# A selective scan cut in two: the decays of one state of each pair move to PSUM, and the edge weights share a bank with C's copies

## The chip, the cores and the metric

The kernel runs on one core of a Trainium2 chip. The metric is the device time of one execution in microseconds (us), as the median of a few runs. Kernels are compared on the same chip.

## What is computed

The reference is one graph layer followed by a mixture of experts, over 6250 nodes of 256 features and 200,000 edges. Only two parts of it run in the stretch that the change touches, side by side.

The first is the graph attention sum: for every edge a row of the projected table is fetched by its source node, scaled by a weight for each of four heads, and added to the row of its target node.

```python
e = leaky_relu(s_src[src] + s_tgt[tgt], 0.2)
agg = segment_sum(proj[src] * attn[:, :, None], tgt)
```

The second is a selective scan ("mamba") over the nodes, sorted by degree, with 256 channels and 16 states:

```python
dA = exp(dt[:, :, None] * A)
dBx = (dt * xc)[:, :, None] * Bm[:, None, :]
h = dA_t * h + dBx_t          # for each t in order
y_t = h @ C_t
```

## The kernel before

`streams` (L510) runs both parts interleaved. The nodes are cut into 28 chunks of 224. A chunk takes 16 **slots**, one for each state. The position of a slot in its chunk is `at` (0 to 15). Two states make a pair: the even slot holds the scan of both, the odd slot what follows from it. The edges come in **edge pairs** of 512 edges (`S` in the code); three slots of every four (`at % 4` = 1, 2, 3) have one, so a chunk has 12. Four edge pairs form a group (`GU = 4`), whose logits and weights are computed together, in the slots with `at` = 1, 6 and 11. `run` writes out 32 slots (two chunks) and loops over them. The order of the work on each engine is written by hand, and engines meet only through semaphores.

What each engine does in a slot, in its order of issue:

- **VectorE**, `slot` L1185: at `at` = 2 `give_out`; `add` (L620: adds the sums of edge pair S-3 from PSUM `fl_ps` to `ACC`); `scale` (L610: multiplies the gathered rows of S-1 by the weights in PSUM `fl_pw`); in a slot that begins a group the first step of `logits` (L585); then in an even slot `scan` (L1124, one instruction over both states, 2 x 2 x 225 = 900 elements: decays `mb_dA`, inflow `mb_dB`, state `mb_h`), in an odd slot `read_out` (L1134: `mb_h` times C from PSUM `fl_pc`, into `mb_hc`); the rest of `logits` (L589 to L602); `prepare` for the next chunk; and in an odd slot `inflow` (L1111: `mb_dB` of the next pair, from PSUM `fl_pb`).
- **ScalarE**, `slot` L1309: `one_hot` (L628, L633), `keep_last` in odd slots (L1239, L1242), `weights` (L648), `give_out`, `prepare`, `decay(M + 2)` (L1251, two instructions of 224 elements for one state), `keep_turned` (L643, L644), and in a slot that begins a group `weights_again` (L654, writes `fl_pw`).
- **TensorE**, `slot` L1440: in an even slot `copies_c` (L1363: spreads two rows of C over all partitions into `fl_pc`), in an odd slot `copies_b` (L1353, the same for B into `fl_pb`); then `edges_tensor`: `gather_sums` of S-2 (L683), `turn` (L663) and `spread` (L670); in an odd slot `sum_up` (L1375); then `give_out` and `prepare` for the next chunk: at `at` = 2 the projection for z (L1382), at `at` = 4 the convolution (L1407).
- **GpSimd**: nothing but the gathers, four indirect DMAs for each edge pair (L567), as far ahead as buffers are free. SyncE brings indices and rows.

All eight PSUM banks are in use: `fl_ptx`, two `fl_ps`, `fl_pw`, `fl_pb`, `fl_pc`, `fl_py`, `fl_pm`. The decays live in SBUF in `mb_dA` with four buffers, one for each state.

Of the kernel before, what the change touches and what calls it, by code (L numbers as in the profile page):

```python
# [7 lines left out]
ALU = mybir.AluOpType  # L8
ACT = mybir.ActivationFunctionType
# [6 lines left out]
P = 128  # L16
# [5 lines left out]
KD = D // P  # L22
NH, FO = 4, 64
ROW = D + NH
SC = 512
NJ = SC // P
# [4 lines left out]
GU = 4  # L31
# [5 lines left out]
NS, DR, CONV = 16, 16, 4  # L37
N2 = NS // 2
TC, RB = 224, 112
# [67 lines left out]
def two_states(m):  # L107

    return Slot(m.i, m.n // 2, BODY // 2)


def pair_beside(m):

    at = m.n % 4 - 1
    return Slot(m.i, G_INTRO + m.n // 4 * 3 + at, GB) if at >= 0 else None
# [395 lines left out]
def streams(nc, sem, w, a, dram, srcT, parts, tile_of):  # L511
# [12 lines left out]

        "weights", "set", "rate", "x", "xT", "xT_sb", "in", "z_in", "z_sb", "history", "xc",
        "bx", "bx_hi", "bx_rest", "bx_mid", "bx_mid_sb", "bx_lo", "dt_row", "dt_in", "v", "abs", "e", "ln", "series",
        "dt", "u", "B", "C", "dA", "dB", "h", "h0", "hc", "y", "skip", "gated", "o", "o_sb", "oT", "oT_sb", "stored")}
    gathered = [sem(f"fl_gathered{g}") for g in range(2 * GU)]
    index = [sem(f"fl_index{h}") for h in range(2)]
    brought = [sem(f"fl_dst{g}") for g in range(4)]  # L530
    early = lambda v, least: isinstance(v, int) and v < least
    with ExitStack() as ctx:
# [19 lines left out]
        pX = pTX[:, words:words + NJ * SPREAD].rearrange("p (j s) -> p j s", s=SPREAD)  # L552
        pS = [ps(f"fl_ps{b}", [P, 512])[:, 0:ROW] for b in range(2)]
        pW = ps("fl_pw", [P, 512])
        weight = pW[:, 0:GU * NJ * NH].rearrange("p (c h) -> p c h", h=NH)
        ACC = w["ACC"]

        def free(pool, p):
# [46 lines left out]
        def scale(dve, p):  # L605
            q, n = p.number, p.n
            g, at = n // GU % 2, slice(n % GU * NJ, (n % GU + 1) * NJ)
            dve.wait_ge(s["weight"], p.of(GU) + 1)
            rows = G[g][:, at, 0:D].rearrange("p j (h f) -> p j h f", h=NH)
            nc.vector.tensor_tensor(rows, rows, weight[:, at, :].unsqueeze(3).to_broadcast([P, NJ, NH, FO]),  # L610
                                    ALU.mult).then_inc(s["scaled"], 1)

        def add(dve, p):
            q = p.number
            k = dve.value_load(tile_of[0:1, bass.ds(q, 1)], min_val=0, max_val=NT - 1)
            at = ACC[:, bass.ds(k, 1), :].rearrange("p o d -> p (o d)")
            if not early(q, 1):
                dve.wait_ge(s["added"], q)
            dve.wait_ge(s["summed"], q + 1)
            nc.vector.tensor_tensor(at, at, pS[p.n % 2], ALU.add).then_inc(s["added"], 1)  # L620
# [29 lines left out]
        def weights_again(act, p):  # L650

            if not early(p.number, 1):
                act.wait_ge(s["scaled"], p.number)
            nc.scalar.activation(weight, DM[:], ACT.Exp).then_inc(s["weight"], 1)  # L654
# [47 lines left out]
        def edges_tensor(pe, S):  # L702
            if not early(S.number, 2):
                gather_sums(pe, S - 2)
            turn(pe, S + GU)
            spread(pe, S + GU)
# [104 lines left out]
        with ExitStack() as part:  # L811
# [14 lines left out]
            first = G_COUNT + 5  # L826
# [101 lines left out]
        with ExitStack() as part:  # L928
# [19 lines left out]
            H0, ZERO = sb("mb_h0", [P, N2, 2, KD]), sb("mb_zero", [P, 1])  # L948
            LOWER = sb("mb_lower", [P, 1])
            Y, O, OR = sb("mb_y", [P, KD, TC]), sb("mb_o", [P, KD, TC]), sb("mb_or", [RB, TS, D])  # L950
            pB, pC = ps("fl_pb", [P, 2, TC]), ps("fl_pc", [P, 2, TC])
            pY, pM = ps("fl_py", [P, KD, TC]), ps("fl_pm", [P, 512])
            wide = lambda t: t[:, 0:KD * TC].rearrange("p (k t) -> p k t", k=KD)
            xs = dram["sorted_x"].rearrange("(c r p) d -> c p r d", p=RB, r=TS)
# [124 lines left out]
            def _(dve):  # L1079
# [19 lines left out]

                nc.vector.memset(LOWER[:], float(-np.log(ROOT)))  # L1100
                nc.vector.memset(dA[:, :, :, 0:1], 0.0).then_inc(s["set"], 1)

                def inflow(p):

# [9 lines left out]
                def scan(p):  # L1114

                    m, n = p.number, p.n
                    dve.wait_ge(s["dB"], m + 1)
                    dve.wait_ge(s["dA"], 2 * m + 2)
                    if not early(m, 1):

                        dve.wait_ge(s["h0"], 2 * m)
                        dve.wait_ge(s["hc"], m)
                    line = lambda t: t.rearrange("p s k t -> p (s k t)")
                    nc.vector.tensor_tensor_scan(line(H[:]), line(dA[:, n % 2 * 2:n % 2 * 2 + 2]), line(dB[:]), ZERO[:, 0:1],  # L1124
                                                 ALU.mult, ALU.add).then_inc(s["h"], 1)

                def read_out(p):
                    m, n = p.number, p.n
                    dve.wait_ge(s["h"], m + 1)
                    dve.wait_ge(s["C"], m + 1)  # L1130
                    if not early(m, 2):

                        dve.wait_ge(s["y"], m - 1)
                    nc.vector.tensor_tensor(HC[:, n % 2], H[:, :, :, 1:], pC[:].unsqueeze(2).to_broadcast([P, 2, KD, TC]), ALU.mult  # L1134
                                            ).then_inc(s["hc"], 1)

                def prepare(c, b, at):
# [47 lines left out]
                def slot(M, S):  # L1185
                    n, c = M.n, M.of(NS)
                    at, b = n % NS, n // NS % 2
                    two = two_states(M)
                    if at == 2 and not early(c, 1):
                        give_out(c - 1, 1 - b)  # L1190
                    if S:
                        add(dve, S - 3)
                        scale(dve, S - 1)
                    steps = logits(dve, S) if S and S.n % GU == 0 else None
                    if steps:
                        next(steps)
                    if at % 2:
                        read_out(two)
                    else:
                        scan(two)  # L1200
                    if steps:
                        next(steps)
                        next(steps)
                        next(steps)
                        next(steps)
                    prepare(c + 1, 1 - b, at)
                    if at % 2:
                        inflow(two + 1)
# [6 lines left out]
                        prepare(0, 0, at)  # L1215
                inflow(two_states(Slot(0, 0)))
                nc.vector.memset(dB[:, :, :, 0:1], 0.0).then_inc(s["set"], 1)
                dve.wait_ge(s["set"], 13)
                run(dve, slot)
                add(dve, pair(PAIRS - 3))  # L1220
                scale(dve, pair(PAIRS - 1))
# [8 lines left out]
            def _(act):  # L1230
                act.wait_ge(s["weights"], 144)
                nc.scalar.activation(AE[:], A[:], ACT.Exp).then_inc(s["rate"], 1)
                act.wait_ge(s["set"], 12)

                def keep_last(p):

# [7 lines left out]
                def decay(p):  # L1244

                    m, n = p.number, p.n
                    if not early(m, 4):

                        act.wait_ge(s["h"], two_states(p).number - 1)
                    for k in range(KD):  # L1250
                        ins = nc.scalar.activation(dA[:, n % 4, k, 1:], DT[:, n // NS % 2, k, :], ACT.Exp,  # L1251
                                                   scale=A[:, k, n % NS:n % NS + 1])
                    ins.then_inc(s["dA"], 1)

# [54 lines left out]
                def slot(M, S):  # L1309
                    n, c = M.n, M.of(NS)  # L1310
                    at, b = n % NS, n // NS % 2
                    if S:
                        one_hot(act, S + (GU + 1))
                    if at % 2:
                        keep_last(two_states(M))
                    if S and S.n % GU == 0:
                        weights(act, S)
                    if not early(c, 1):
                        give_out(c - 1, at)
                    prepare(c + 1, 1 - b, at)  # L1320
                    decay(M + 2)
                    if S:
                        keep_turned(act, S + GU)
                    if S and S.n % GU == 0:
                        weights_again(act, S)

                for k in range(SCAT):
# [12 lines left out]
            def _(pe):  # L1340
# [16 lines left out]
                def copies_c(p):  # L1357

                    m, n = p.number, p.n
                    if not early(m, 1):  # L1360
                        pe.wait_ge(s["hc"], m)
                    for r in range(2):
                        mm = nc.tensor.matmul(pC[:, r, :], SEL[:, NS + 2 * (n % N2) + r, :], PARTS[:, n // N2 % 2, :],  # L1363
                                              start=True, stop=True, skip_group_check=True)
                    mm.then_inc(s["C"], 1)
# [74 lines left out]
                def slot(M, S):  # L1440
                    n, c = M.n, M.of(NS)
                    at, b = n % NS, n // NS % 2
                    two = two_states(M)
                    if at % 2:
                        copies_b(two + 1)
                    else:
                        copies_c(two)
                    if S:
                        edges_tensor(pe, S)
                    if at % 2 and not early(M.number, 2):  # L1450
                        sum_up(two - 1)
                    if not early(c, 1):
                        give_out(c - 1, at)
                    prepare(c + 1, 1 - b, at)
# [862 lines left out]
```

## Time and profile before

| | |
|---|---|
| median of 3 runs | 3823.23 us (3822.45 to 3824.71) |
| profiled execution, own time | 3830.27 us |
| its span, first to last instruction | 3828.5 us |
| mean granted TensorE clock | 0.898 of full speed |
| 28 chunks of slots | from about 912 to 2872 us of the span |

The profile is of one execution. In a row of grouped instructions stand the line, the engine, the operation, what it writes and reads, how many, and then busy time in us, the mean of one in ns, and the idle time of the engine just before them with what ended it. In a row of the timeline stand the start and the duration in us, and in brackets the idle time just before, where there was any. Consecutive VectorE rows overlap a little: the next one starts some 0.08 us before the recorded end of the one before.

### The profile page before, as it was taken

The page shows a single profiled execution, that of the slowest core. Times are in us where ns is not written, and L with a number is a line of the kernel's source. Part 1 is how long each engine was busy: PE and PEld are TensorE (multiplying, and loading weights), DVE is VectorE, ACT ScalarE, POOL GpSimd, SP SyncE. Part 2 cuts the span into 40 slices and gives each one's busy share as a digit, 9 for nine tenths or more (in the row PEclk, how much of TensorE's full clock was granted, in tenths as well). Part 3 has the DMA queues.
Part 4 walks back from the last instruction along what each step waited for, and adds up shares of the span by engine and source line. Part 5 has one row for each costly group of instructions (what it writes and reads, how often), then busy time and mean ns, then how long its engine had stood idle before and what let it go on. Part 6 is the DMA issues. An engine that isn't in the chain of part 4 may idle for free. (4 is left out here: it accounts for less than half of the span.)

```text
span 3828.5 us, 60997 instructions
## 1 busy us (share of the span) xinstructions
PE 2897.5 (76%) x16306; PEld 2157.1 (56%) x16307; DVE 2661.2 (70%) x4225; ACT 2163.9 (57%) x4819; POOL 2649.2 (69%) x2119
## 2 busy tenths in 40 slices
PE   6465566517888788887888888888883889659998
PEld 5455455415565565565665655656652455448887
DVE  6577466625988988989888888899893788511111
ACT  2322377716777677777676776777772665412222
POOL 2788788877777777777777777777773477424443
PEclk9788777768899999999999999999996999879999
DMA  7333444454444444544444444444465243157775
GB/s 225 105 83 84 133 106 107 115 172 131 118 124 121 124 118 117 127 120 122 124 118 120 123 118 126 121 120 124 120 112 136 56 106 99 69 133 143 143 144 105
DMA packets 295783, 460.78 MB, mean 120 GB/s; under 512 B 59431, under 2 KB 217880, under 8 KB 295288
## 3 DMA queue, kind: packets, MB, share of 16 engines
q0 software_dynamic: 116320, 279.61, 30.8%
q1 hardware_dynamic: 179224, 178.73, 16.6%
q14 instruction: 180, 1.47, 0.1%
q8 instruction: 59, 0.97, 0.1%
HBM read 394.01 MB, written 63.43 MB: 119 GB/s over the span
## 5 line engine op out<-in xcount | busy, mean ns | idle before, releaser
L567 POOL DMA_INDIRECT el_g<-table,el_ix x1344 | 1546.7, 1151 | 412.4 <-issue 392.9
L683 PE MATMUL fl_ps<-el_g,el_oh 128*128 128x260 f32 x3520 | 959.0, 420 | 255.2 <-DVE el_g L610 207.2
L683 PEld LDWEIGHTS fl_ps<-el_g,el_oh 128*128 128x128 f32 x3520 | 697.3, 209 | 370.5 <-DVE el_g L610 215.1
L567 POOL DMA_INDIRECT el_g<-table,eg_src x436 | 592.8, 1360 | 155.2 <-issue 125.9
L610 DVE TENSOR_TENSOR el_g<-el_g,fl_pw 128x1024 f32<-128x1024 f32 x440 | 533.5, 1213 | 22.2 <-ACT fl_pw L654 22.1
L1124 DVE TENSOR_TENSOR_SCAN mb_h<-mb_dA,mb_zero,mb_dB 128x900 f32<-128x900 f32 x224 | 468.1, 2090 | 51.2 <-ACT mb_dA L1251 30.7
L1375 PE MATMUL fl_py<-mb_hc,ident 128*128 128x448 f32 x896 | 405.0, 576 | 0.5 <-DVE mb_hc L1134 0.5
L1251 ACT ACTIVATE mb_dA<-mb_dt,mb_a 128x224 f32<-128x224 f32 x900 | 382.7, 475 | 35.3 <-issue 21.2
L628 ACT ACTIVATE el_away<-el_dst,el_less 128x512 bf16<-128x512 bf16 x445 | 321.1, 721 | 108.3 <-DMA el_dst<-dst_rows 81.3
L2258 POOL DMA_INDIRECT out<-ex_y,ex_to x112 | 174.2, 1555 | 279.3 <-DVE ex_y L2217 254.5
L643 ACT CAST el_oh<-fl_ptx 128x512 f32<-128x512 bf16 x444 | 253.6, 571 | 190.8 <-PE fl_ptx L670 185.6
L663 PE MATMUL fl_ptx<-el_ident,el_oht 128*128 128x128 bf16 x1776 | 183.9, 230 | 183.3 <-ACT el_sx L644 167.3
L633 ACT ACTIVATE el_oht<-el_away 128x512 bf16<-128x512 bf16 x445 | 280.3, 630 | 36.2 <-issue 5.4
L663 PEld LDWEIGHTS fl_ptx<-el_ident,el_oht 128*128 128x128 bf16 x1776 | 139.5, 103 | 283.4 <-issue 155.0
L1111 DVE TENSOR_TENSOR mb_dB<-mb_u,fl_pb 128x896 f32<-128x896 f32 x225 | 242.5, 1078 | 46.8 <-PE fl_pb L1353 46.8
L2217 DVE TENSOR_TENSOR ex_y<-ex_py,ex_b 128x512 f32<-128x512 f32 x56 | 38.8, 692 | 333.0 <-PE ex_py L2179 333.0
L648 ACT ACTIVATE el_g<-el_dm 128x64 f32<-128x64 f32 x110 | 28.2, 256 | 424.6 <-DVE el_dm L601 424.4
L620 DVE TENSOR_TENSOR ACC<-ACC,fl_ps 128x260 f32 x440 | 182.7, 415 | 115.9 <-PE fl_ps L683 78.1
L1134 DVE TENSOR_TENSOR mb_hc<-mb_h,fl_pc 128x896 f32<-128x896 f32 x224 | 241.6, 1078 | 0.0
L585 DVE TENSOR_REDUCE el_s<-el_sx 128x128 f32<-128x384 f32 x110 | 67.6, 615 | 233.7 <-DMA el_g<-table,eg_src 171.3
L2232 ACT COPY ex_xt<-ex_px 128x512 f32<-128x512 f32 x56 | 32.8, 586 | 345.2 <-PE ex_px L2153 345.2
L1363 PE MATMUL fl_pc<-mb_parts,mb_sel 96*128 96x224 bf16 x448 | 84.9, 272 | 167.0 <-DVE mb_hc L1134 167.0
(306 smaller groups left out, 5509.0 us busy)
## 6 DMA issues: line engine op xcount, KB each, us to landing
el_dst<-dst_rows SPq DMA_DIRECT2D x446, 128.0 KB, 3.4
ex_w<-in_moe_W SPq DMA_DIRECT2D x56, 512.0 KB, 3.4
el_g<-table,el_ix POOLq DMA_INDIRECT x1344, 3.0
ex_x<-routed_x SPq DMA_DIRECT2D x56, 257.0 KB, 2.8
el_g<-table,eg_src POOLq DMA_INDIRECT x436, 2.8
mb_x<-sorted_x SPq DMA_DIRECT2D x30, 224.0 KB
table<-px_tr SPq DMA_DIRECT2D x7, 910.0 KB, 9.6
el_g<-in_x SPq DMA_DIRECT2D x7, 896.0 KB, 8.0
```

Of the source, the lines that this page charges most:

```text
L567: pool.indirect_dma_start(out=G[b // GU][:, b % GU * NJ + j, :], out_offset=None, in_=dram["table"], in_offset=bass.IndirectOffsetOnAxis(a ...
L610: nc.vector.tensor_tensor(rows, rows, weight[:, at, :].unsqueeze(3).to_broadcast([P, NJ, NH, FO]), ALU.mult).then_inc(s["scaled"], 1)
L628: nc.scalar.activation(AWAY[:], DST[:, n % 4, :], ACT.Abs, bias=LESS[:, 0:1]).then_inc(s["away"], 1)
L633: nc.scalar.activation(OHT[:, n % RO, :], AWAY[:], ACT.Relu, bias=1.0, scale=-1.0).then_inc(s["hot"], 1)
L643: nc.scalar.copy(OH[:, n % (2 * GU)], pT)
L663: nc.tensor.transpose(pT[:, j, :], OHT[:, n % RO, j * P:(j + 1) * P], I16[:])
L683: mm = nc.tensor.matmul(pS[n % 2], OH[:, n % (2 * GU), j, :], G[n // GU % 2][:, n % GU * NJ + j, :], start=j == 0, stop=j == NJ - 1)
L1111: nc.vector.tensor_tensor(dB[:, :, :, 1:], wide_u, pB[:].unsqueeze(2).to_broadcast([P, 2, KD, TC]), ALU.mult).then_inc(s["dB"], 1)
L1124: nc.vector.tensor_tensor_scan(line(H[:]), line(dA[:, n % 2 * 2:n % 2 * 2 + 2]), line(dB[:]), ZERO[:, 0:1], ALU.mult, ALU.add).then_inc(s[ ...
L1134: nc.vector.tensor_tensor(HC[:, n % 2], H[:, :, :, 1:], pC[:].unsqueeze(2).to_broadcast([P, 2, KD, TC]), ALU.mult).then_inc(s["hc"], 1)
L1251: ins = nc.scalar.activation(dA[:, n % 4, k, 1:], DT[:, n // NS % 2, k, :], ACT.Exp, scale=A[:, k, n % NS:n % NS + 1])
L1375: mm = nc.tensor.matmul(pY[:], w["ident"][:], HC[:, n % 2, r], start=first and r == 0, stop=last and r == 1)
```

## The change

Five edits, all in this stretch:

1. The edge weights (`fl_pw`) move to the upper half of a bank, and C's copies to its lower half. The bank that is freed holds `pA`, one buffer of decays for the first state of each pair.
2. `decay` writes the first state of a pair to `pA` in PSUM and the second to `mb_dA` in SBUF (two buffers). Since `pA` is single, the order becomes `decay(M + 3)` in even slots and `decay(M + 1)` in odd ones, and the first state's decay waits for the first half of the scan that read `pA` last.
3. The scan is two instructions of 450 elements: the first reads its decays from `pA`, the second from `mb_dA`.
4. On TensorE `copies_c` moves from the front of the even slot to behind `edges_tensor`, and waits until the `scale` of the same slot is done (and, after a group's first pair, until its weights are written).
5. VectorE waits for C's copies before `scale` in odd slots, and ScalarE waits before `weights_again` for C's copies (even slots) or for `read_out` (odd slots).

```diff
-        weight = pW[:, 0:GU * NJ * NH].rearrange("p (c h) -> p c h", h=NH)
+        weight = pW[:, 2 * TC:2 * TC + GU * NJ * NH].rearrange("p (c h) -> p c h", h=NH)
...
-            pB, pC = ps("fl_pb", [P, 2, TC]), ps("fl_pc", [P, 2, TC])
+            pB, pC = ps("fl_pb", [P, 2, TC]), pW[:, 0:2 * TC].rearrange("p (r t) -> p r t", r=2)
+            pA = ps("fl_pa", [P, 512])[:, 0:1 * KD * (1 + TC)].rearrange("p (s k t) -> p s k t", s=1, k=KD)
...
-                    line = lambda t: t.rearrange("p s k t -> p (s k t)")
-                    nc.vector.tensor_tensor_scan(line(H[:]), line(dA[:, n % 2 * 2:n % 2 * 2 + 2]), line(dB[:]), ZERO[:, 0:1],
+                    line = lambda t: t.rearrange("p k t -> p (k t)")
+                    nc.vector.tensor_tensor_scan(line(H[:, 0]), line(pA[:, 0]), line(dB[:, 0]), ZERO[:, 0:1],
+                                                 ALU.mult, ALU.add).then_inc(s["first"], 1)
+                    nc.vector.tensor_tensor_scan(line(H[:, 1]), line(dA[:, n % 2]), line(dB[:, 1]), ZERO[:, 0:1],
                                                  ALU.mult, ALU.add).then_inc(s["h"], 1)
...
                     if S:
                         add(dve, S - 3)
+                        if at % 2:
+                            dve.wait_ge(s["C"], two.number + 1)
                         scale(dve, S - 1)
...
-                    if not early(m, 4):
-
-                        act.wait_ge(s["h"], two_states(p).number - 1)
+                    if n % 2:
+                        to = dA[:, n // 2 % 2]
+                        if not early(m, 4):
+
+                            act.wait_ge(s["h"], two_states(p).number - 1)
+                    else:
+                        to = pA[:, 0]
+                        if not early(m, 2):
+
+                            act.wait_ge(s["first"], two_states(p).number)
                     for k in range(KD):
-                        ins = nc.scalar.activation(dA[:, n % 4, k, 1:], DT[:, n // NS % 2, k, :], ACT.Exp,
+                        ins = nc.scalar.activation(to[:, k, 1:], DT[:, n // NS % 2, k, :], ACT.Exp,
                                                    scale=A[:, k, n % NS:n % NS + 1])
...
-                    decay(M + 2)
+                    decay(M + 1 if at % 2 else M + 3)
                     if S:
                         keep_turned(act, S + GU)
                     if S and S.n % GU == 0:
+
+                        act.wait_ge(s["hc"] if at % 2 else s["C"], two_states(M).number + 1)
                         weights_again(act, S)
...
                     if at % 2:
                         copies_b(two + 1)
-                    else:
-                        copies_c(two)
                     if S:
                         edges_tensor(pe, S)
+                    if not at % 2:
+
+                        last = S or pair_beside(M - 1)
+                        pe.wait_ge(s["scaled"], last.number)
+                        if not S and last.n % GU == 0:
+
+                            pe.wait_ge(s["weight"], last.of(GU) + 1)
+                        copies_c(two)
```

## Rows read from the trace of the kernel before

**Rows 1.** The page: busy us, share of the span and instructions of each engine.
```profile
PE 2897.5 (76%) x16306; PEld 2157.1 (56%) x16307; DVE 2661.2 (70%) x4225; ACT 2163.9 (57%) x4819; POOL 2649.2 (69%) x2119
```

**Rows 2.** Windows: all 28 chunks, then chunks of 71.3 us and 69.1 us; PEclk, DMA share, GB/s last.
```profile
912.00:2872.00 1960.00, 1624.79 (x8948) 1173.49 (x8948) 1737.47 (x2298) 1410.97 (x3448) 1547.50 (x1345) 0.96 0.48 121
...
1191.91:1263.19 71.28, 58.62 (x321) 42.36 (x321) 62.08 (x82) 52.13 (x127) 56.04 (x51) 0.95 0.49 123
1263.19:1332.29 69.10, 56.37 (x317) 41.27 (x316) 61.99 (x83) 48.30 (x120) 54.78 (x48) 0.98 0.47 121
```

**Rows 3.** Timeline of GpSimd around two scans of VectorE.
```profile
2111.91 0.95 POOL L567 DMA_INDIRECT el_g<-table,el_ix  x1 [0.30 <-issue]
2113.16 2.25 POOL L567 DMA_INDIRECT el_g<-table,el_ix  x1 [0.30 <-issue]
...
2119.47 1.71 POOL L567 DMA_INDIRECT el_g<-table,el_ix  x1 [0.30 <-issue]
```

**Rows 4.** Grouped instructions of GpSimd, 1100 to 2800 us.
```profile
L567 POOL DMA_INDIRECT el_g<-table,el_ix x1167 | 1344.6, 1152 | 355.7 <-issue 338.6 <-PE fl_ps L683 17.1
```

**Rows 5.** Timeline of VectorE from `scale` in slot 2 to `inflow` in slot 5.
```profile
2111.44 1.21 DVE L610 TENSOR_TENSOR el_g<-el_g,fl_pw 128x1024 f32<-128x1024 f32 x1
2112.57 2.09 DVE L1124 TENSOR_TENSOR_SCAN mb_h<-mb_dA,mb_zero,mb_dB 128x900 f32<-128x900 f32 x1
2114.57 0.40 DVE L620 TENSOR_TENSOR ACC<-ACC,fl_ps 128x260 f32 x1
...
2118.33 2.09 DVE L1124 TENSOR_TENSOR_SCAN mb_h<-mb_dA,mb_zero,mb_dB 128x900 f32<-128x900 f32 x1 [0.23 <-DVE mb_dB L1111]
...
2123.84 1.09 DVE L1111 TENSOR_TENSOR mb_dB<-mb_u,fl_pb 128x896 f32<-128x896 f32 x1 [0.98 <-PE fl_pb L1353]
```

**Rows 6.** Grouped instructions of VectorE, 1100 to 2800 us.
```profile
L1124 DVE TENSOR_TENSOR_SCAN mb_h<-mb_dA,mb_zero,mb_dB 128x900 f32<-128x900 f32 x194 | 405.2, 2089 | 43.5 <-ACT mb_dA L1251 26.6 <-DVE mb_dB L1111 16.9
L610 DVE TENSOR_TENSOR el_g<-el_g,fl_pw 128x1024 f32<-128x1024 f32 x292 | 354.2, 1213 | 15.4 <-ACT fl_pw L654 15.4
L1134 DVE TENSOR_TENSOR mb_hc<-mb_h,fl_pc 128x896 f32<-128x896 f32 x195 | 210.3, 1078 | 0.0
...
L585 DVE TENSOR_REDUCE el_s<-el_sx 128x128 f32<-128x384 f32 x73 | 44.9, 615 | 20.8 <-ACT el_sx L644 12.7 <-DMA el_g<-table,el_ix 7.8
...
L1180 DVE SCALAR_TENSOR_TENSOR mb_y<-mb_xc,mb_dp,fl_py 128x224 f32<-128x224 f32 x48 | 19.2, 441 | 0.0
...
L1169 DVE TENSOR_TENSOR mb_u<-mb_dt,mb_xc 128x448 f32<-128x448 f32 x25 | 15.6, 626 | 3.2
```

**Rows 7.** The wait before L1111 in two chunks: 1193 to 1262 us, then 1265 to 1331 us.
```profile
L1111 DVE TENSOR_TENSOR mb_dB<-mb_u,fl_pb 128x896 f32<-128x896 f32 x8 | 8.6, 1078 | 2.9 <-PE fl_pb L1353 2.9
...
L1111 DVE TENSOR_TENSOR mb_dB<-mb_u,fl_pb 128x896 f32<-128x896 f32 x8 | 8.6, 1078 | 1.0 <-PE fl_pb L1353 1.0
```

**Rows 8.** Timeline of TensorE over the same slots, from the C copies of slot 2.
```profile
2107.59 0.36 PE L1363 MATMUL fl_pc<-mb_parts,mb_sel 96*128 96x224 bf16 x2
...
2110.73 0.38 PE L663 MATMUL fl_ptx<-el_ident,el_oht 128*128 128x128 bf16 x4 [1.01 <-ACT el_sx L644]
...
2111.71 1.76 PE L1382 MATMUL fl_pm<-mb_xt,mb_wi 128*128 128x224 f32 x8
...
2117.18 0.36 PE L1363 MATMUL fl_pc<-mb_parts,mb_sel 96*128 96x224 bf16 x2
2117.38 2.45 PE L1407 MATMUL fl_pm<-mb_xt,mb_wc 128*128 128x224 f32 x12
...
2123.45 0.36 PE L1353 MATMUL fl_pb<-mb_parts,mb_sel 96*128 96x224 bf16 x2
```

**Rows 9.** Timeline of TensorE, the C copies of slot 14 in another chunk.
```profile
2023.05 0.36 PE L1363 MATMUL fl_pc<-mb_parts,mb_sel 96*128 96x224 bf16 x2 [3.12 <-DVE mb_hc L1134]
```

**Rows 10.** Grouped instructions of ScalarE, 1100 to 2800 us: the same exponent, into SBUF and into PSUM.
```profile
L648 ACT ACTIVATE el_g<-el_dm 128x64 f32<-128x64 f32 x73 | 18.7, 256 | 200.9 <-DVE el_dm L601 200.7
L654 ACT ACTIVATE fl_pw<-el_dm 128x64 f32<-128x64 f32 x73 | 17.6, 241 | 0.0
```

More of the change, by code:

```diff
@@ L526, in streams @@
         "bx", "bx_hi", "bx_rest", "bx_mid", "bx_mid_sb", "bx_lo", "dt_row", "dt_in", "v", "abs", "e", "ln", "series",
-        "dt", "u", "B", "C", "dA", "dB", "h", "h0", "hc", "y", "skip", "gated", "o", "o_sb", "oT", "oT_sb", "stored")}
+        "dt", "u", "B", "C", "dA", "dB", "h", "first", "h0", "hc", "y", "skip", "gated", "o", "o_sb", "oT", "oT_sb", "stored")}
     gathered = [sem(f"fl_gathered{g}") for g in range(2 * GU)]
@@ L1101, in _ @@
                 nc.vector.memset(dA[:, :, :, 0:1], 0.0).then_inc(s["set"], 1)
+                nc.vector.memset(pA[:, :, :, 0:1], 0.0).then_inc(s["set"], 1)
                 def inflow(p):
@@ L1133, in read_out @@
                         dve.wait_ge(s["y"], m - 1)
-                    nc.vector.tensor_tensor(HC[:, n % 2], H[:, :, :, 1:], pC[:].unsqueeze(2).to_broadcast([P, 2, KD, TC]), ALU.mult
+                    nc.vector.tensor_tensor(HC[:, n % 2], H[:, :, :, 1:], pC.unsqueeze(2).to_broadcast([P, 2, KD, TC]), ALU.mult
                                             ).then_inc(s["hc"], 1)
@@ L1217, in _ @@
                 nc.vector.memset(dB[:, :, :, 0:1], 0.0).then_inc(s["set"], 1)
-                dve.wait_ge(s["set"], 13)
+                dve.wait_ge(s["set"], 14)
                 run(dve, slot)
@@ L1232, in _ @@
                 nc.scalar.activation(AE[:], A[:], ACT.Exp).then_inc(s["rate"], 1)
-                act.wait_ge(s["set"], 12)
+                act.wait_ge(s["set"], 13)
                 def keep_last(p):
```

## The prediction

> **What bounds the kernel now.** I read the page first: no engine is busy all of the span [rows 1]. The windows say where to look: the 28 chunks take 1960 of 3828.5 us, and in them VectorE is busy 1737 (89%), TensorE 1625 (83%), GpSimd 1547 (79%) [rows 2]. The change touches nothing outside.
>
> GpSimd is fuller than 79%. A gather takes 0.95 us when left alone, with 0.30 us of issue before it [rows 3], but the mean is 1152 ns, and of its 356 us idle 339 are that 0.30 [rows 4]: it never really waits. The difference comes from the scans. The gather at 2113.16 began 0.59 us into the scan at 2112.57 and took 2.25 us; the next scan began at 2118.33 and the gather at 2119.47, 1.14 us into it, took 1.71 [rows 3, 5]. Both gathers end 2.84 to 2.85 us after the scan's start. So a gather that starts during a scan stands until it ends, then takes 0.76 us. That costs up to 1.8 us (2.85 - 0.1 - 0.95), less the later it starts; over the 1167 gathers it is 1167 x 0.20 = 236 us, or 1.2 us for each of 194 scans. `scale`, which reads weights from PSUM, does no such thing: the gather at 2111.91 ran beside it in 0.95.
>
> But who paces? A chunk needs 48 x 1.25 + 8 x 1.2 = 69.6 us on GpSimd. Chunks take 69.1 us at a mostly full clock and 71.3 where the clock falls to its lower level (1.2 GHz) in the wrong place [rows 2]. So both are at the edge. What GpSimd costs VectorE shows as waits for gathered rows: 7.8 us in 1700 [rows 6], 9 us over the stage. VectorE's 62 us of work a chunk [rows 2] is surrounded by waits of another kind, in one place: `inflow` of slot 5 waits for TensorE's B, 1.0 us at full clock, 2.9 after a fall of the clock [rows 7]. TensorE has no pause from the projection of slot 2 (2111.71) over `sum_up` and the convolution to that B (2123.45) [rows 8]. In slots 2 to 5 TensorE sets the pace, in the light slots 9 to 1 VectorE does.
>
> **The copies of C, moved.** In slot 2 of every chunk TensorE did C at 2107.59, ahead of a pause of 1.01 us in which `turn` waits for ScalarE [rows 8]; there it cost nothing. Now C stands behind `spread` and waits for `scale` of slot 2, which ends at 2112.65 [rows 5]. With some 0.06 us for a semaphore to pass (my assumption, below anything that matters here) and 0.20 from C's start to the next matmul (2117.18 to 2117.38), the projection starts at 2112.91, not 2111.71: **1.20 us later**. Queued behind it are B and `gather_sums` of slot 3, `sum_up`, C of slot 4, the convolution and B of slot 5, back to back, and `inflow` already waits for that. `gather_sums` of slot 2 can start earlier, but `turn` behind it still waits for ScalarE, so nothing comes back. Cost 28 x 1.18 = **33 us** (the same difference over 26 chunks is 1.18 on average). Upper bound: the same. Lower bound: zero, if ScalarE's turn or the scale came elsewhere.
>
> Elsewhere the move is covered. In slots 6, 10 and 14 TensorE's C needs the `scale` of its slot, but VectorE's next user is `scale` of the odd slot, a scan (2.0) and an add later [rows 5], and TensorE needs 0.36. In slot 12 C waits for the group's weights, written behind `keep_turned` of slot 11, which I estimate at 1 to 2 us later than now; TensorE has 3 us free there, before C of slot 14 [rows 9]. The new wait of ScalarE stands behind `keep_turned`, two copies long, and C is one 0.36 us matmul pair behind the same `spread`. Were that cover gone, each would cost under 0.4 us, in one slot of 16.
>
> **The scan in two.** 900 elements take 2089 ns [rows 6]. L1134 and L610 show 135 ns for 128 elements more, 1.05 each; at twice 1.04 for a scanned one (an estimate: no second size of scan is in the trace) 1875 are elements and 214 are fixed; L1180, which like the scan takes a scalar by pointer, has 441 - 234 = 207 fixed [rows 6]. A half is 1.15 us and starts its successor 0.08 earlier, so two occupy 2.14 instead of 2.01 (2112.57 to 2114.57): **+0.13 us** a scan. Bounds: 0.06 with the fixed 143 of a plain operation, 0.22 if nothing overlaps. Scans of slots 2 and 4 lie inside the wait of slot 5 (1.0 us, 2.2 after the move); six of eight count: 28 x 6 x 0.13 = **22 us** (10 to 37).
>
> Does reading decays from PSUM cost? L1134 with one PSUM operand has 1078 - 933 = 145 fixed, L1169 with both in SBUF 626 - 467 = 159 [rows 6]. I take nothing. The Trainium skill ("VectorE: DVE Perf Modes", the errata section) states 120 cycles fixed from PSUM against 58 from SBUF; by that each first half would be 0.065 us longer, 11 us in all. The rows show no such difference.
>
> **The decays.** The same two instructions per slot, half of them into PSUM. The exponent into PSUM took 241 ns, into SBUF 256 [rows 10]; gain 0.03 us a state, relevant only where scan 8 waits for ScalarE (1.1 us a chunk, part of the 26.6 [rows 6]): under 1 us in all. The last decay of a pair is issued in the same odd slot as now, and its new wait, for a first half one slot back, has long ended.
>
> **The gathers.** Only the second half still reads two SBUF tensors. A gather then stands for at most 1.15 us instead of 2.09; of a period of 1.25 us the mean stall falls from 1.2 to 0.3 us. GpSimd's chunk falls to 48 x 1.25 + 8 x 0.3 = 62.4 us, and its waits vanish: **-9 us**. If both halves still stopped gathers, GpSimd's 69.6 would lie under the new 71 anyway, so the same.
>
> **Sum.** 33 + 22 - 9 = +46 us on the profiled 3830.3, which is 7 above the median of 3823.2. One more item: TensorE's pause ahead of slot 2's `turn` grows from 1.0 to some 3 us, since `gather_sums` runs earlier, right before the stretch that sets the pace; about a third of the chunks lose 1.9 us there to the lower clock now [rows 7], and I add a tenth of the chunks more (+5) within -17 (none fall) and +25. The forecast is 3823 + 51 = **3874 us**.
>
> **Rivals.**
> - *GpSimd paces* (faster). For it: its 69.6 us a chunk is the chunk's length, and it never waits. Against it: chunks as short as 69.1 with VectorE hardly waiting for rows. If its relief is worth the whole gap from 70.0 (1960 / 28) down to VectorE's 62 plus 5 of its other waits, plus 8 x 0.13, a chunk is 68.0, 56 us gained; with the C move still there 33 of it goes: 3800. It decides if the C wait has to be under 1 us a chunk and the row waits are larger than the 7.8 that the trace names. The Trainium skill ("SBUF — State Buffer", on the two sides) has the rule behind it: VectorE with two SBUF inputs and GpSimd exclude each other from a shared port pair for the whole instruction. The stalls agree (1.71 and 2.25 against 0.95).
> - *C is hidden* (slower, less). The wait of slot 5 absorbs it, or `scale` of slot 2 comes earlier than TensorE gets there: 22 - 9 = +13, 3836.
> - *The clock falls oftener* (slower, more). The longer pause makes most chunks 71.3 or more: 18 x 1.9 = 34 above the sum, 3903.
> - *No change*: the scan's halves at their lower bound (28 x 6 x 0.06 = 10) cancel the relief, and C is hidden: 3824.
>
> **Numbers.** Forecast 0.60; C hidden 0.14; clock 0.12; GpSimd 0.09; no change 0.05. The range, 3832 to 3900, leaves out GpSimd, no change, and the end of the clock case. A change of 0.2% (7.6 us) is about what the measurement tells from none: slower 0.85, same 0.06, faster 0.09.
>
> **What would show it.** L1363 of slot 2 starts 0.06 us after that slot's L610 ends, L1382 behind it; L1111 of slot 5 waits about 2 us at full clock; scans of 450 elements at 1.15 us each; gathers beside first halves at 0.95 and none above 2.2; no wait of L610 for C; chunks near 71 us. I am wrong if a PSUM scan costs more or less than 1.15, if slot 5's B is not what TensorE's chain ends in, or if chunks drop under 70.

## The result, and the profile after

The changed kernel takes 3900.26 us (median of 4 runs, 3897.23 to 3903.16) against 3823.44 for the kernel before on the same chips: a ratio of 1.0201 (95% interval 1.0183 to 1.0218), 77 us slower. The forecast was 3874 us, slower, with 3832 to 3900 as the range: the sign was right, the time lies just outside the range, 0.3 us above its upper end, and the loss was 77 us where 51 were forecast. The profiled execution took 3897.23 us, its span is 3895.2.

The page shows the relief of GpSimd at once (2649 us busy before, 2455 after), while VectorE has 21 us more:

```profile
span 3895.2 us, 61688 instructions
...
PE 2927.2 (75%) x16306; PEld 2182.6 (56%) x16307; DVE 2682.6 (69%) x4450; ACT 2163.0 (56%) x4819; POOL 2454.7 (63%) x2119
```

The first and the last scan of the stage, from one view of each kernel's `mb_h`, give the length of a chunk: 27.875 chunks lie between them. Before:

```profile
L1124 DVE TENSOR_TENSOR_SCAN mb_h<-mb_dA,mb_zero,mb_dB x224: 2080/2091/2157, 915.1 to 2865.5; 128x900 f32<-128x900 f32 x112
```

After (numbers behind the count are the shortest, median and longest in ns, then the first and the last start in us):

```profile
L1126 DVE TENSOR_TENSOR_SCAN mb_h<-fl_pa,mb_zero,mb_dB x224: 1139/1152/1156, 914.7 to 2939.2; 128x450 f32<-128x450 f32 x112
```

That is 69.97 us before and 72.63 after, 2.66 us a chunk and 74 us over the stage. The loss lies in it: outside the stage the traced execution after is 7 us shorter than the one before, and the latter took 7 us more than its kernel's median.

Grouped instructions after, 1100 to 2800 us, the counterparts of [rows 6, 4, 10]:

```profile
L1126 DVE TENSOR_TENSOR_SCAN mb_h<-fl_pa,mb_zero,mb_dB 128x450 f32<-128x450 f32 x187 | 215.0, 1150 | 37.7 <-ACT fl_pa L1264 21.5 <-DVE mb_dB L1113 16.2
L1128 DVE TENSOR_TENSOR_SCAN mb_h<-mb_dA,mb_zero,mb_dB 128x450 f32<-128x450 f32 x188 | 212.6, 1131 | 0.0
L1113 DVE TENSOR_TENSOR mb_dB<-mb_u,fl_pb 128x896 f32<-128x896 f32 x188 | 202.8, 1078 | 84.7 <-PE fl_pb L1368 84.7
L585 DVE TENSOR_REDUCE el_s<-el_sx 128x128 f32<-128x384 f32 x70 | 42.9, 613 | 13.2 <-ACT el_sx L644 13.2
...
L567 POOL DMA_INDIRECT el_g<-table,el_ix x1127 | 1136.9, 1009 | 564.7 <-issue 317.1 <-PE fl_ps L683 247.6
...
L1264 ACT ACTIVATE mb_dA<-mb_dt,mb_a 128x224 f32<-128x224 f32 x374 | 159.0, 476 | 49.8 <-DVE mb_h L1128 49.5
L1264 ACT ACTIVATE fl_pa<-mb_dt,mb_a 128x224 f32<-128x224 f32 x376 | 153.8, 441 | 10.8 <-DVE mb_dt L1169 10.5
```

Four things are to be seen. The halves cost 1150 and 1131 ns, as forecast. The gathers fell from 1152 to 1009 ns, GpSimd now waits 248 us for buffers that TensorE frees, and the 7.8 us of waits for gathered rows before L585 are gone. But the wait of `inflow` for B, all of it in slot 5 (single chunks of before in [rows 7]), has grown from 39.6 us to 84.7. The same group before, and one matmul group each of the slot 2 projection before and after:

```profile
L1111 DVE TENSOR_TENSOR mb_dB<-mb_u,fl_pb 128x896 f32<-128x896 f32 x194 | 209.1, 1078 | 39.6 <-PE fl_pb L1353 39.6
...
L1382 PE MATMUL fl_pm<-mb_xt,mb_wi 128*128 128x224 f32 x192 | 51.3, 419 | 0.0
```

```profile
L1397 PE MATMUL fl_pm<-mb_xt,mb_wi 128*128 128x224 f32 x184 | 71.6, 570 | 0.0
```

The chain that leads to it, in TensorE's timeline from `gather_sums` of slot 2, beside [rows 8]:

```profile
2078.47 2.00 PE L683 MATMUL fl_ps<-el_g,el_oh 128*128 128x260 f32 x8
2083.38 0.38 PE L663 MATMUL fl_ptx<-el_ident,el_oht 128*128 128x128 bf16 x4 [2.91 <-ACT el_sx L644]
2084.28 0.27 PE L670 MATMUL fl_ptx<-eg_parts,el_oht 128*128 x4 [0.52 <-issue]
2085.36 0.55 PE L1378 MATMUL fl_pw<-mb_parts,mb_sel 96*128 96x224 bf16 x2 [0.80 <-DVE el_g L610]
2085.71 3.22 PE L1397 MATMUL fl_pm<-mb_xt,mb_wi 128*128 128x224 f32 x8
2088.72 0.58 PE L1368 MATMUL fl_pb<-mb_parts,mb_sel 96*128 96x224 bf16 x2
2089.09 2.96 PE L683 MATMUL fl_ps<-el_g,el_oh 128*128 128x260 f32 x8
```

VectorE's `scale` in slot 2 and in slot 5 of the same chunk:

```profile
2084.09 1.21 DVE L610 TENSOR_TENSOR el_g<-el_g,fl_pw 128x1024 f32<-128x1024 f32 x1
...
2094.20 1.22 DVE L610 TENSOR_TENSOR el_g<-el_g,fl_pw 128x1024 f32<-128x1024 f32 x1 [0.60 <-PE fl_pw L1378]
```

The order is what the prediction drew: C (L1378) starts 0.06 us after `scale` of slot 2 ended at 2085.30 and the projection follows. But the projection takes 3.22 us, not 1.76, and `gather_sums` of slot 3 takes 2.96, not 1.93. The windows name the cause (the column behind POOL is the granted clock): 0.56 in the stretch that holds them, so for most of it the lower level of 1.2 GHz.

```profile
2078.00:2085.00 7.00, 3.13 (x18) 1.85 (x16) 6.55 (x15) 5.55 (x17) 5.48 (x6) 0.95 0.46 121
2085.00:2092.00 7.00, 6.64 (x22) 5.49 (x23) 6.77 (x8) 3.82 (x11) 4.45 (x5) 0.56 0.63 149
```

In the 7 us ahead TensorE was busy 3.1. How often the clock falls there can be counted by the length of this projection: at a full clock its eight records take 1.7 to 1.8 us, and in the kernel before 11 of the 28 in the stage took over 1.9 us, after the change all 28. The average time of one of its matmuls says the same: 353 to 362 ns where the projection never meets a lower clock (below), 419 before, 570 after. `inflow` of slot 5 waits 1.0 us in the chunks of before without a fall of the clock and 2.5 to 2.9 in the 11 with one; after the change it waits 3.2 to 4.1 in every chunk.

One sign of the prediction did not hold: it expected no wait of `scale` for C. With the chain at the lower clock the C copies of slot 4 come late too, and `scale` of slot 5 waits for them in every fourth chunk, 0.60 us here and 3.7 us in all from 1100 to 2800 us. With the clock held (experiment 9) that wait is gone.

### The profile page after: what moved, and what is told of

It is laid out like the page before. It is cut to its first block and busy times, and to the rows that moved or that the text cites. A ratio compares the mean times of both kernels' runs of the same rounds, so it can differ in the third digit from the quotient of the medians.

```text
span 3895.2 us, 61688 instructions
## 1 busy us (share of the span) xinstructions
PE 2927.2 (75%) x16306; PEld 2182.6 (56%) x16307; DVE 2682.6 (69%) x4450; ACT 2163.0 (56%) x4819; POOL 2454.7 (63%) x2119
## 5 line engine op out<-in xcount | busy, mean ns | idle before, releaser
L567 POOL DMA_INDIRECT el_g<-table,el_ix x1344 | 1353.6, 1007 | 675.1 <-issue 384.2
L1390 PE MATMUL fl_py<-mb_hc,ident 128*128 128x448 f32 x896 | 393.1, 562 | 0.3 <-DVE mb_hc L1138 0.3
L1126 DVE TENSOR_TENSOR_SCAN mb_h<-fl_pa,mb_zero,mb_dB 128x450 f32<-128x450 f32 x224 | 257.5, 1150 | 45.6 <-ACT fl_pa L1264 24.3
L1128 DVE TENSOR_TENSOR_SCAN mb_h<-mb_dA,mb_zero,mb_dB 128x450 f32<-128x450 f32 x224 | 253.3, 1131 | 0.0
L1138 DVE TENSOR_TENSOR mb_hc<-mb_h,fl_pw 128x896 f32<-128x896 f32 x224 | 241.6, 1078 | 0.0
L1264 ACT ACTIVATE mb_dA<-mb_dt,mb_a 128x224 f32<-128x224 f32 x450 | 191.2, 476 | 54.3 <-DVE mb_h L1128 54.0
L585 DVE TENSOR_REDUCE el_s<-el_sx 128x128 f32<-128x384 f32 x110 | 67.5, 614 | 222.4 <-DMA el_g<-table,eg_src 169.1
```

What stands on the lines that cost most here:

```text
L567: pool.indirect_dma_start(out=G[b // GU][:, b % GU * NJ + j, :], out_offset=None, in_=dram["table"], in_offset=bass.IndirectOffsetOnAxis(a ...
L1126: nc.vector.tensor_tensor_scan(line(H[:, 0]), line(pA[:, 0]), line(dB[:, 0]), ZERO[:, 0:1], ALU.mult, ALU.add).then_inc(s["first"], 1)
L1128: nc.vector.tensor_tensor_scan(line(H[:, 1]), line(dA[:, n % 2]), line(dB[:, 1]), ZERO[:, 0:1], ALU.mult, ALU.add).then_inc(s["h"], 1)
L1138: nc.vector.tensor_tensor(HC[:, n % 2], H[:, :, :, 1:], pC.unsqueeze(2).to_broadcast([P, 2, KD, TC]), ALU.mult).then_inc(s["hc"], 1)
L1390: mm = nc.tensor.matmul(pY[:], w["ident"][:], HC[:, n % 2, r], start=first and r == 0, stop=last and r == 1)
```

## The experiments

All ran against the kernel before on the same chip; ratios are to it, with 95% intervals. "Chunk" is worked out as above, "wait for B" is the idle time before `inflow` that TensorE's B ended, "projection" the mean of one matmul of the slot 2 projection, these two from 1100 to 2800 us. "Falls" is how many of the 28 projections in the stage took over 1.9 us. Chunk, wait, projection and falls come from one traced execution of each kernel.

| kernel | ratio | chunk, us | wait for B, us | projection, ns | falls |
|---|---|---|---|---|---|
| before | 1 | 69.97 | 39.6 | 419 | 11 |
| changed | 1.0201 | 72.63 | 84.7 | 570 | 28 |
| 1 scan in two only | 1.0071 | 70.86 | 35.4 | 429 | 12 |
| 2 C and the bank only | 1.0139 | 71.88 | 81.4 | 546 | 28 |
| 3 changed, pause put back | 1.0168 | 72.43 | 81.5 | 550 | 26 |
| 4 changed, C behind the projection | 1.0085 | 71.30 | 55.3 | 501 | 24 |
| 5 changed, decays in SBUF | 1.0198 | 72.85 | 86.9 | 577 | 28 |
| 6 edits 3 and 4 | 1.0049 | 70.78 | 45.8 | 466 | 16 |
| 7 before, with filler | 0.9985 | 69.93 | 31.6 | 362 | 0 |
| 8 edit 4, with filler | 0.9976 | 69.75 | 23.2 | 362 | 0 |
| 9 changed, with filler | 1.0052 | 70.66 | 45.2 | 353 | 0 |
| 10 edit of 1, with filler | 1.0020 | 70.26 | 19.3 | 362 | 0 |

### 1. The scan in two, and nothing else

```diff
-                    nc.vector.tensor_tensor_scan(line(H[:]), line(dA[:, n % 2 * 2:n % 2 * 2 + 2]), line(dB[:]), ZERO[:, 0:1],
+                    nc.vector.tensor_tensor_scan(line(H[:, 0]), line(dA[:, n % 2 * 2]), line(dB[:, 0]), ZERO[:, 0:1],
+                                                 ALU.mult, ALU.add)
+                    nc.vector.tensor_tensor_scan(line(H[:, 1]), line(dA[:, n % 2 * 2 + 1]), line(dB[:, 1]), ZERO[:, 0:1],
                                                  ALU.mult, ALU.add).then_inc(s["h"], 1)
```

> The kernel before with the scan alone cut in two, both halves reading their decays from SBUF. Theory (the scan costs its second start, and nothing else of the change is here): the two halves occupy 2.11 to 2.14 us where one took 2.01; six scans of eight count in a chunk, 28 x 6 x 0.11 = +18 us, less some row waits that vanish as the chunks grow: 3833 to 3842. A gather is still stopped by both halves. Rival (the cut itself upsets more, for instance each half is stopped by GpSimd in turn): +35 us or more, 3860.

1.0071 (1.0046 to 1.0095): 27 us, between the theory and its rival. The scans behave as expected (a median of 1153 ns; from the first half's start to the next instruction 2.11 to 2.21 us instead of 2.00 to 2.09, 0.11 more in most slots), which is 18 us in the six slots that count. The rest lies in one place: before `add` of slot 13 VectorE stands 1.15 us instead of 0.32 in every second chunk, with no releaser named ("issue"). The same instruction in a chunk with the stall and in the next, without it:

```profile
1679.55 0.42 DVE L620 TENSOR_TENSOR ACC<-ACC,fl_ps 128x260 f32 x1 [1.15 <-issue]
...
1749.56 0.42 DVE L620 TENSOR_TENSOR ACC<-ACC,fl_ps 128x260 f32 x1 [0.31 <-issue]
```

Slots are written out for two chunks and looped, so it is a fixed place in VectorE's program; what it is was not found. The changed kernel does not have it, nor has experiment 5, whose scans are cut in the same way from SBUF. GpSimd gained here too, though both halves read two SBUF tensors:

```profile
L567 POOL DMA_INDIRECT el_g<-table,el_ix x1152 | 1225.8, 1064 | 474.8 <-issue 322.5 <-PE fl_ps L683 152.3
```

### 2. C and the shared bank, and nothing else

The edits to `weight`, `pC`, TensorE's slot and the two waits as in the change; scan and decays as before.

> The kernel before with the weights and C's copies in one bank, and all the order and waits that come with it; the scan stays one instruction from SBUF, the decays as before. Theory (the move costs 1.33 us a chunk on TensorE's chain, and by the longer pause ahead of it the clock falls in every chunk, 1.1 us a chunk more): 28 x 2.45 = 68, less the 9 of row waits that vanish: 3880 to 3888, L1111 of slot 5 waits some 3.7 us. Rival (the clock falls because of the new decays or scans, the move costs its matmul shift alone): 3850. Rival (GpSimd, not relieved here, paces once the chunk is disturbed): 3900 or more, with row waits before L585.

1.0139 (1.0114 to 1.0163), 53 us, 3877.61 us. The wait for B is 81.4 us and the projection 546 ns: the added falls of the clock come with this part of the change (28 of 28 chunks), and not from decays or scans (12 in experiment 1, 11 before). GpSimd is hardly relieved (1151 ns a gather) and does not pace: no wait for rows before L585. Together with 18 us for the scans this leaves 6 us of the change's 77; as measured, with the stall of experiment 1, the two parts make 80. It missed the lower end of the expectation by 2 us.

### 3. The pause put back

```diff
                     if S:
+                        if at % 2 == 0:
+                            pe.wait_ge(s["hc"], two.number)
                         edges_tensor(pe, S)
```

> The changed kernel with one wait more: in slots 2, 6, 10 and 14 TensorE begins its edge work only when read_out of the slot before is done, as it did by accident when C's copies stood in front. No work is added. Theory (the clock falls in every chunk because gather_sums runs too early and leaves a pause of 3 us ahead of turn): the falls at slot 2 go back to less than half of the chunks, 15 to 31 us gained: 3870 to 3885. Rival (the falls come from the new 0.8 us pause behind spread, or from anything else): a fall in every chunk still, 3900.

1.0168 (1.0144 to 1.0192), a gain of 12 us by the two ratios, whose intervals overlap, and the projection still at 550 ns with a fall in 26 chunks of 28. My reason for the falls, that `gather_sums` runs too early, fell with it as the only one: alone it decides little.

### 4. C behind the projection

```diff
+                    if at == 2:
+                        prepare(c + 1, 1 - b, at)
                     if not at % 2:
...
                         copies_c(two)
...
-                    prepare(c + 1, 1 - b, at)
+                    if at != 2:
+                        prepare(c + 1, 1 - b, at)
```

> The changed kernel with C's copies of slot 2 behind the projection of slot 2 instead of ahead of it; all waits stay. Theory (the projection and all behind it wait 0.8 us for scale plus the copies themselves): the projection starts right behind spread, 1.1 us earlier, and C costs 0.2 us on the chain: 28 x 1.1 = 31 gained, 3869, with the clock falling in every chunk as before or a little less. Rival (TensorE's chain of slots 2 to 5 is not what paces; the clock alone does): 3895 to 3900.

1.0085 (1.0059 to 1.0111): 44 us of the 77 are back by the place of one pair of small matmuls. More than the 31 expected, since the clock improves too (501 ns, 24 falls instead of 28).

### 5. The decays back in SBUF

The change with `mb_dA` in four buffers and `decay(M + 2)` as before, so without the use of the freed bank.

> The changed kernel with all decays back in SBUF, four buffers and their old order; C moved, bank shared, scan in two. It is the change without what the freed bank is used for. Theory (GpSimd does not pace at 72 us a chunk; where the decays lie is worth nothing): within 8 us of the changed kernel, 3892 to 3908, with gathers again stopped by both halves, so GpSimd near 67 us of a chunk. Rival (relief of GpSimd hides part of the cost): 3915 or more, with row waits before L585.

1.0198 (1.0181 to 1.0215), the same as the change. Its chunks are 0.22 us longer in the one trace of each, and an exponent takes 475 ns where it takes 441 into PSUM; the ratios do not tell the two kernels apart. For GpSimd the bank is worth 1009 instead of 1045 ns a gather, and nothing waits for that.

### 6. Both edits, 3 and 4

> Both edits in one: gather_sums of the even slots waits for read_out, and C of slot 2 stands behind the projection. In slot 2 TensorE then does what it did before the change, but for C (0.2 us). Theory now (the clock falls because of all pauses ahead of the projection together: 3 us ahead of turn, 0.5 ahead of spread, 0.8 ahead of C): the falls at slot 2 go back to about half of the chunks, 10 to 20 us under the C-behind run: 3838 to 3850. Rival (a fall in slot 2 follows from what TensorE does at other times, for example the later slots): a fall in every chunk, 3855 to 3862.

1.0049 (1.0032 to 1.0065), 3848.26 us. The projection is at 466 ns, and the order in slot 2 is that of the kernel before but for C. Falls in 28 chunks with both pauses, 26 and 24 with one of them gone, 16 with both gone: each pause ahead of the projection has its share, and together they count for more than one by one. These are counts of one trace each.

### 7 to 9. Filler

If pauses of TensorE make the clock fall, work for nothing in them must hold it. Five matmuls go into the pause ahead of `turn` in slot 2; they write to `fl_pm`, where the projection overwrites them, so the result is unchanged (each is two records in the trace):

```diff
+                    def filler():
+                        pe.wait_ge(s["xT_sb"], c + 2)
+                        for _ in range(5):
+                            nc.tensor.matmul(wide(pM)[:, 0, :], WI[:, 0, D:D + P], XT[:, 0, CONV - 1:], start=True,
+                                             stop=True, skip_group_check=True)
...
-                        edges_tensor(pe, S)
+                        edges_tensor(pe, S, filler if at == 2 else None)
```

> The kernel before with five matmuls of 128x224 in slot 2, between gather_sums and turn, into fl_pm, where the projection then overwrites them: work for nothing, in TensorE's pause of 1 us. Theory (9 of 22 chunks lose some 1.9 us in slots 2 to 5 to the lower clock, which follows from pauses of TensorE ahead of them): the falls at slot 2 go, 10 to 21 us gained, 3801 to 3813. Rival (the clock does not decide, or filler of this kind does not hold it): 3822 to 3830, the filler costs up to 0.3 us a chunk.

> The C-behind kernel with the same five matmuls in slot 2. Theory (clock): falls at slot 2 go from nearly every chunk to few; the chain of slots 2 to 5 is 1 to 1.7 us shorter: 20 to 40 us gained on the C-behind run, 3820 to 3840. Rival: 3855 to 3865.

> The changed kernel with the five filler matmuls in slot 2, ahead of turn, and C left where the change put it. It splits the loss of slot 2 into its parts. Theory (two parts that add: the lower clock, and the projection that waits for scale and C): falls at slot 2 become few, L1111 of slot 5 waits some 2.0 us instead of 3.7, a chunk is 70.9 us, 45 us gained on the changed kernel: 3850 to 3862; what then remains against the kernel with C behind and filler, some 30 us, is the wait for scale. Rival (the 0.8 us pause behind spread is enough for the clock to fall): falls in most chunks, 3880 or more.

In the changed kernel (9) the filler gives back three quarters of the loss: 1.0201 becomes 1.0052 (1.0035 to 1.0069), and a chunk 70.66 us instead of 72.63. That is 57 us where 45 were expected, and 3843 us lies below the expected 3850 to 3862; `inflow` of slot 5 now waits 1.8 to 2.1 us. TensorE in slot 2, the filler first:

```profile
2047.85 2.16 PE L1464 MATMUL fl_pm<-mb_xt,mb_wi 128*128 128x224 f32 x10 [1.39 <-ACT mb_xt L1275]
2049.86 0.38 PE L663 MATMUL fl_ptx<-el_ident,el_oht 128*128 128x128 bf16 x4
2050.22 0.26 PE L670 MATMUL fl_ptx<-eg_parts,el_oht 128*128 x4
2051.30 0.37 PE L1380 MATMUL fl_pw<-mb_parts,mb_sel 96*128 96x224 bf16 x2 [0.82 <-DVE el_g L610]
2051.50 1.69 PE L1399 MATMUL fl_pm<-mb_xt,mb_wi 128*128 128x224 f32 x8
```

The 0.82 us wait for `scale` is still there, the clock is full and the projection is back at 1.7 us:

```profile
2051.00:2058.00 7.00, 6.70 (x39) 5.45 (x40) 6.77 (x8) 6.05 (x16) 5.19 (x6) 1.00 0.55 143
```

With C behind the projection as well (8), no wait is left in slot 2 behind the filler, a chunk is 69.75 us, and the kernel is faster than the one before: 3818.39 us, 0.9976 (0.9966 to 0.9987), about 9 us; against experiment 4 that is 42 us, where 20 to 40 were expected. From 9 to 8, 0.91 us a chunk or 25 us, is what the place ahead of the projection costs when the clock is out of it.

In the kernel before (7) the filler keeps the clock of the projection (419 to 362 ns), but the wait for B falls only from 39.6 to 31.6 us, where 1.0 us a chunk would be 24, and the gain is 6 us, 0.9985 (0.9976 to 0.9995): little more than half of the least that I expected. The 3825.04 us lie in the rival's 3822 to 3830, though the kernel before took 3829.58 on that chip. Two things took the rest. The first: in five chunks behind the first one the clock falls all the same, but earlier, behind a pause of 1.8 to 2.1 us ahead of C's copies, and `inflow` of slot 5 waits 2.4 to 2.6 us. One of them, TensorE in slot 2 (`gather_sums` takes 3.05 us instead of 1.93, the filler 2.75 instead of 2.1):

```profile
1476.41 0.36 PE L1365 MATMUL fl_pc<-mb_parts,mb_sel 96*128 96x224 bf16 x2 [1.98 <-DVE mb_hc L1136]
1476.70 3.05 PE L683 MATMUL fl_ps<-el_g,el_oh 128*128 128x260 f32 x8
1479.54 2.75 PE L1449 MATMUL fl_pm<-mb_xt,mb_wi 128*128 128x224 f32 x10
...
1482.45 1.76 PE L1384 MATMUL fl_pm<-mb_xt,mb_wi 128*128 128x224 f32 x8
```

The second is GpSimd. The lines of L585 show it, first for 7, then for 8:

```profile
L585 DVE TENSOR_REDUCE el_s<-el_sx 128x128 f32<-128x384 f32 x73 | 44.9, 615 | 25.9 <-DMA el_g<-table,el_ix 15.2 <-ACT el_sx L644 10.5
```

```profile
L585 DVE TENSOR_REDUCE el_s<-el_sx 128x128 f32<-128x384 f32 x74 | 45.4, 614 | 13.7 <-ACT el_sx L644 13.7
```

```profile
L567 POOL DMA_INDIRECT el_g<-table,el_ix x1171 | 1205.2, 1029 | 496.3 <-issue 332.5 <-PE fl_ps L683 163.8
```

In 7 the waits for gathered rows doubled, from 7.8 to 15.2 us; in 8, where GpSimd is relieved (1029 ns a gather, 164 us of waits for buffers), there are none. So GpSimd was indeed the next limit of the kernel before: of the 0.3 us a chunk that the wait for B lost in 7, the waits for rows took nearly all back.

### 10. Is the freed bank needed for that gain?

The split scan of experiment 1 with the same filler, banks as before.

> The kernel before with the scan in two halves from SBUF and the five filler matmuls; banks and C as before. It asks whether the freed bank is needed for the gain of the C-behind kernel with filler (0.9976 of before). Theory (two halves in SBUF already let GpSimd in between, mean stall 0.4 us a scan against 1.1, and no chunk falls at slot 2): a chunk of 69.9 to 70.4 with the 0.8 us stall of slot 13 in every second chunk, 3822 to 3836, a ratio of 0.998 to 1.003. Rival (GpSimd needs the decays in PSUM): row waits before L585 and 3840 or more.

1.0020 (1.0010 to 1.0031). No wait for rows before L585, so two halves in SBUF relieve GpSimd enough. It is 17 us slower than 8. 12 of them are the unexplained stall before slot 13's `add` (0.4 us a chunk on average). That leaves some 5 us for the freed bank together with the move of C that it needs; the scan's waits for decays are 26.6 us here and 22.5 in 8, which is about that much over the stage. Whether the stall has to do with the banks is open, so this 5 is an estimate.

## Why the prediction had the sign right and the time wrong

**The copies of C, moved: right.** 33 us forecast. The projection starts behind `scale` and C as drawn. With the clock out of play the wait for B is 45.2 us in experiment 9 and 19.3 in 10, which has the same halves and filler but C in its old place: 1.9 against 0.8 us a chunk, so the move costs 1.1 us, 30 in all. (9 against 8 gives 25, since behind the projection C still takes 0.2 us of the chain.)

**The scan in two: right.** 22 us forecast (+0.13 us each), 18 found (+0.11 in each of six slots; those of slots 2 and 4 lie in the wait of slot 5, which is 0.8 us in experiment 10 instead of 1.0). The halves last 1.15 and 1.13 us. Reading decays from PSUM costs nothing that can be seen: the first half has a median of 1152 ns with them in PSUM, and of 1153 ns with them in SBUF (experiment 1). The Trainium skill's 120 cycles from PSUM against 58 from SBUF ("VectorE: DVE Perf Modes", errata section) are not borne out by these runs.

**The gathers: right in sum, for another reason than stated.** -9 us forecast; the row waits of 7.8 us in 1700 vanished. But they vanished in every longer chunk, relieved or not (experiment 2). Beside a first half, which reads PSUM, none of the changed kernel's gathers took over 0.95 us, and none at all over 1.82: that part was as drawn.

**The decays: undersized.** 0.03 us a state, "under 1 us in all". They save 35 ns an instruction, and the scan's waits for decays fell from 26.6 us to 21.5 (1.1 to 0.9 us a chunk), 5 us over the stage. In whole times this is not shown: experiment 5 and the change cannot be told apart.

**The clock: the term that failed.** The prediction put +5 us on it, "a tenth of the chunks more", within -17 and +25. It saw the longer pause ahead of slot 2's `turn`, and named the case of most chunks falling as a rival at 3903 with a chance of 0.12. That rival is what happened: all 28 chunks fall, against 11 before, and the time is 3900. Experiment 9 sizes the falls in slots 2 to 5 of the changed kernel at 1.97 us a chunk; those of the kernel before cost 0.63 (39.6 us of waits in 24.3 chunks, less the 1.0 of a chunk without a fall). The difference, 1.34 us a chunk, is 37 us, not 5. Two things were missed. The pause of 0.8 us behind `spread`, which the prediction itself had worked out as part of the C move, is a pause ahead of the same stretch, and experiments 3, 4 and 6 show that both count. And "a tenth" had no row behind it: the term's range ended at +25, below the +34 that the prediction had worked out for its own rival. The range of the forecast left out the end of that case, and the time fell there.

The parts then add up: 37 for the clock, 30 for C, 18 for the scans, less 9 for rows and 5 for decays, are 71, against 74 in the stage and 77 by the ratio. The few us between are not assigned. The four terms beside the clock give 34, where 46 were forecast for them. It is luck that this excess of 12 hid part of the 32 by which the clock term fell short.

**GpSimd paces: wrong as a rival, right as the next limit.** It did not turn the sign, since the chain of slots 2 to 5 grew by far more. But with that chain cured the relief shows: the filler is worth 6 us to the kernel before, whose waits for rows double, and the changed kernel with the filler and with C behind the projection is the fastest of all.

## What to carry to other kernels

A small instruction moved behind a wait on an in-order queue costs what stands behind it, not its own 0.36 us; look for a place behind the long work instead of ahead of it. Before TensorE work that sets the pace, count each pause that an edit adds or lengthens, and read the granted clock of the stretch behind it: here 1.9 us added to one pause and a new one of 0.8 us cost about as much as everything else in the change, and five matmuls without a purpose won the clock's part back. Filler in one pause does not cover the next: in the kernel before some falls only moved ahead of it. Where two engines are within 1% of each other, curing one shows little until the other is cured too.

## What the runs showed of the hardware that was not expected

- TensorE was busy 3.1 of 7 us ahead of the projection, the granted clock behind it was 0.56, and the same matmuls took 3.22 instead of 1.76 us. With the pause filled the clock stayed at 1.00, although a pause of 0.82 us remained.
- A gather is stopped by a half scan of two SBUF tensors as by a whole one, but gets in between two halves: the mean of all gathers is 1152 ns in the kernel with whole scans (the longest in the stage 2.75 us), 1064 with two halves in SBUF (1.83), 1009 with the first half reading from PSUM (1.82).
- An exponent over 224 elements takes 476 ns into SBUF and 441 into PSUM; with 64 elements the difference was 15 ns [rows 10].
- The scan cut in two in the kernel before came with a stall of 0.84 us at a fixed place in every second chunk (experiment 1); experiment 5 and the changed kernel have as many scans and no such stall, and its cause stays open.
